# One graph-attention kernel: decoding of the next group, the last product of a group and two element-wise operations moved in the order of work

## The chip, the cores and the metric

The kernel runs on one core of a Trainium2 chip. The metric is the device time in microseconds (us) of one execution. The engines are TensorE (PE in the rows; PEld is its loading of weights), VectorE (DVE), ScalarE (ACT), GpSimd (POOL) and SyncE (SP), which only starts transfers here. Each follows its own list of instructions in order, and they meet at semaphores: an instruction that waits holds up all that is behind it on its engine.

## The reference

```python
scores = (x @ W @ a1)[:, None] + (ent @ W @ a2)[None, :]      # 4096 x 4096
e = where(scores > 0, scores, 0.2 * scores)
e = where(adj > 0, e, -9e15)                                  # adj: int32, 4096 x 4096
h = softmax(e, axis=1) @ ent + x                              # 4096 x 64
out = layernorm(x + elu(h))                                   # over the last axis
```

## The kernel before, in words

The 4096 rows of x are cut into five groups of 4, 6, 8, 8 and 6 tiles of 128 rows; the 4096 entities are 32 blocks of 128. A *step* is one block b of one group g; there are 160 steps. I name a group g0 to g4 and a block b0 to b31. Every group goes through these stages, spread over the group before it and itself:

- **Turning.** GpSimd starts the loads of `adj` (four blocks of a group in one load, five buffers `raw`). TensorE turns two blocks at a time (`turn_pair`, L693) into one of two `pairs` buffers in PSUM. ScalarE, for some pairs VectorE, stores them as `mask` (L315, L511); 44 blocks of mask are kept, so turning runs ahead of the group that uses it. From b20 of group g on, the pairs turned belong to group g+2.
- **Histogram and decoding.** Every stored pair also goes through small matmuls into `hist` (`add_hist`, L709). Once all 16 pairs of the next group are in, ScalarE copies hist (`copy_hist`, L323), TensorE spreads it (`spread_hist`, L724), VectorE finds each row's highest bin and a shift (`decode`, nine instructions from L480 to L500), TensorE makes a row of it (`make_row`, L731), and ScalarE copies the row to `drow` (`take_row`, L340). The first hist matmul of the group after next waits for the copy. The first `masked` of the next group waits for `drow`.
- **Weights.** For two blocks at a time VectorE takes the minimum of mask and drow (`masked`, L522, into `xm`), one block at a time it adds the score (`exponents`, L530), and ScalarE takes the exponential (`weights`, L329). Five buffers `wts` let VectorE be at most four blocks ahead of TensorE.
- **Product.** `weigh` (L744 and L747) multiplies the weights with the entities and sums them, three steps (LAG) behind: at b of the program TensorE does the product of block b-3. One product is eight L744 and six or eight L747 matmuls. The first product of a group waits until ScalarE has copied the sums of the group before (`take_acc`, L348 and L349, at b2).
- **Finish.** Sums and rows are turned back (`turn_sums`, L762; `turn_back`, L772), and VectorE works through twelve parts (`finish`) of the group before, one at some blocks: sum and reciprocal, entity features, multiply, add x, minimum with 0 (L584) and maximum (L585), add ScalarE's exponential (L589), mean (L592), centring (L595), square (L598), sum of squares (L601), scale (L604), and after a power on GpSimd (L272) the last multiplication (L607).

Which part stands at which block is set by the table of numbers at the top of the file. Ahead of the loop stands a prologue: scale and highest value of the scores, then all turning and decoding of g0. In it VectorE reduces the entities (`ent_part`, L615) and then does `find_shift` (L465 to L470), which waits for a small matmul (`p_to_all`, L677); behind both stand its first stored pairs (L511), for which TensorE's later turns wait.

Of the kernel before, what the change touches and what calls it, by code (L numbers as in the profile page):

```python
# [9 lines left out]
NG = len(SIZES)  # L10
# [41 lines left out]
def attention_layernorm(nc, x, adj, ent_blocks, turned_in, weights_in, out):  # L52

# [17 lines left out]
    with ctx:  # L71
# [133 lines left out]
        rstd_done = sem("rstd_done")  # L205
        y_done = sem("y_done")
# [53 lines left out]
        def _(pool):  # L260
# [37 lines left out]
        def _(act):  # L298
# [32 lines left out]
            def elu(g):  # L331
                e_g = e[:, 0:SIZES[g], :]
                act.wait_ge(att_done, g + 1)
                act.activation(e_g, e_g, ACT.Exp).then_inc(elu_done, 1)  # L334
# [21 lines left out]
            for j in range(4, GROUP_PAIRS):  # L356
                store_pair(j)
                if j == 10:
                    p_row(0)
# [3 lines left out]
            for g in range(NG):  # L363
                for b in range(NB):
                    s = NB * g + b
                    if g and b == ACC_AT:
                        take_acc(g - 1)
                    for j in range(made_by(s - 1), made_by(s)):
# [3 lines left out]
                    if g and b == ELU_AT:  # L372
                        elu(g - 1)
                    if g + 1 < NG and b == HIST_COPY_AT:
                        copy_hist(g + 1)
                    if g + 1 < NG and b == DROW_AT:
                        take_row(g + 1)
                    weights(g, b)
            take_acc(NG - 1)
            elu(NG - 1)  # L380

        @block.vector
        def _(dve):
# [184 lines left out]
            def finish(g, part):  # L568
# [10 lines left out]
                elif part == 3:  # L579
                    fin_wait()  # L580
                    fin_inc(dve.tensor_tensor(y_g, y_g, x_gr, ALU.add))
                elif part == 4:
                    fin_wait()
                    dve.tensor_scalar(e_g, y_g, 0.0, None, ALU.min).then_inc(att_done, 1)  # L584
                    fin_inc(dve.scalar_tensor_tensor(y_g, y_g, 0.0, x_gr, ALU.max, ALU.add))  # L585
                elif part == 5:
                    fin_wait()
                    dve.wait_ge(elu_done, g + 1)
                    fin_inc(dve.scalar_tensor_tensor(y_g, e_g, -1.0, y_g, ALU.add, ALU.add))  # L589
# [3 lines left out]
                elif part == 7:  # L593
                    fin_wait()
                    fin_inc(dve.scalar_tensor_tensor(y_g, spread(mean), -1.0 / F, y_g, ALU.mult, ALU.add))  # L595
                elif part == 8:
                    fin_wait()
                    fin_inc(dve.tensor_tensor(e_g, y_g, y_g, ALU.mult))  # L598
                elif part == 9:
                    fin_wait()  # L600
                    fin_inc(dve.tensor_reduce(var[:, 0:n], e_g, AX.X, ALU.add))  # L601
                elif part == 10:
                    fin_wait()
                    dve.tensor_scalar(var[:, 0:n], var[:, 0:n], 1.0 / F, EPS, ALU.mult, ALU.add).then_inc(var_done, 1)  # L604
                else:
# [240 lines left out]
```

## Time and profile before

| | us |
|---|---|
| median of 3 runs | 375.44 (375.23 to 376.32) |
| the profiled execution | 377.46 |
| its span, first to last instruction | 375.4 |
| PE busy | 305.7 (81%) |
| DVE busy | 308.4 (82%) |
| ACT busy | 264.4 (70%) |
| POOL busy | 47.2 (13%) |

The profiled execution took 377.46 us, 2.0 us more than its span. The span divides by the first `masked` of each group: the prologue ends at 45.12 us, g0 at 101.3, g1 at 166.41, g2 at 239.53, g3 at 307.0, and g4 with the rest runs to the end. No engine is busy all the time, but two are above 80%, so what counts is who is waited for in each stage. The granted TensorE clock (PEclk) is 1.00 at the full 2.4 GHz and 0.50 at 1.2 GHz.

### The profile page before, as it was taken

Reading aid. Unit: us, or ns where it says so; the run is one execution under the profiler, and the core shown is the slowest. Engines: PE = TensorE matmul, PEld = TensorE weight load, DVE = VectorE, ACT = ScalarE, POOL = GpSimd, SP = SyncE. Lnnn points to the kernel's source line nnn. Section 1 sums busy time; section 2 is a strip of 40 time slices with the busy share of each in tenths; the row PEclk is TensorE's granted clock in tenths of the full one; section 3 lists DMA queues with packets and bytes.
Section 4 is the critical chain, followed back from the end, with each engine's and each line's share of the span. In section 5 each row is a group of like instructions: output and inputs, shape, how many; then the busy total and the mean of one; then the engine's idle time right before and its main releaser. Section 6 shows DMA issues by size and latency. Waiting matters only on the chain.

```text
span 375.4 us, 9071 instructions
## 1 busy us (share of the span) xinstructions
PE 305.7 (81%) x3920; PEld 163.2 (43%) x3920; DVE 308.4 (82%) x436; ACT 264.4 (70%) x263; POOL 47.2 (13%) x54
## 2 busy tenths in 40 slices
PE   1379599997879999996999979879997767957750
PEld 0356466665545554552545435335442313412220
DVE  1894586863797999569899996799999999999955
ACT  1163299897588989589999975799876568646530
POOL 5012111110101001400100041000000500000201
PEclk9999879998989999998999989999999999999995
DMA  7999999999977940999665009940000000000000
GB/s 151 251 206 174 186 200 161 205 207 208 188 119 115 151 74 2 144 208 209 103 91 81 0 3 168 205 72 0 2 2 2 2 28 3 3 0 2 0 30 22
DMA packets 35240, 37.32 MB, mean 99 GB/s; under 512 B 832, under 2 KB 34432, under 8 KB 35200
## 3 DMA queue, kind: packets, MB, share of 16 engines
q0 software_dynamic: 33408, 33.56, 56.3%
q1 hardware_dynamic: 1792, 3.18, 3.0%
q8 instruction: 31, 0.51, 0.5%
q14 instruction: 9, 0.07, 0.1%
HBM read 69.24 MB, written 1.05 MB: 187 GB/s over the span
## 4 chain that ended last, share of the span: by engine, by line
PE 35%; DVE 27%; issue 23%; ACT 11%; DMA 2%; POOL 1%; POOLq 0%; DVEq 0%; SPq 0%; ACTq 0%
PE acc L744 13%; PE pairs L693 10%; DVE xm L522 8%; DVE wts L530 7%; PE acc L747 6%; ACT mask L315 5%; ACT wts L329 3%; PE hist L709 3%; DMA ent_sb<-ent_blocks_dram 2%; DVE y L563 1%; PE misc L668 1%; ACT drow L340 1%; DVE ent_part L615 1%; PE misc L724 1%; POOL rstd L272 1%
## 5 line engine op out<-in xcount | busy, mean ns | idle before, releaser
L329 ACT ACTIVATE wts<-wts,q_bias 128x768 f32<-128x768 f32 (+2 forms) x160 | 152.1, 976 | 56.1 <-DVE wts L530 55.9
L744 PE MATMUL acc<-wts,ent_sb 128*32 128x384 f32 (+2 forms) x1280 | 152.5, 525 | 28.3 <-ACT wts L329 19.4
L530 DVE SCALAR_TENSOR_TENSOR wts<-pb,q_bend,xm 128x768 f32<-128x768 f32 (+2 forms) x160 | 167.5, 1070 | 8.2 <-PE acc L747 7.7
L315 ACT ACTIVATE mask<-pairs 128x2048 bf16<-128x2048 bf16 (+2 forms) x67 | 104.3, 1559 | 35.8 <-PE pairs L693 35.5
L747 PE MATMUL acc<-wts,onesf 128*32 128x256 f32 (+1 forms) x1152 | 93.2, 362 | 0.0
L522 DVE TENSOR_TENSOR xm<-mask,drow 128x1536 bf16<-128x1536 bf16 (+2 forms) x80 | 80.8, 1010 | 9.9 <-ACT drow L340 9.9
L693 PE MATMUL pairs<-ident,raw 128*128 128x128 bf16 x1024 | 79.5, 235 | 1.8 <-ACT mask L315 0.9
L693 PEld LDWEIGHTS pairs<-ident,raw 128*128 128x128 bf16 x1024 | 65.2, 106 | 27.9 <-issue 27.5
L747 PEld LDWEIGHTS acc<-wts,onesf 128*32 128x32 f32 x1152 | 41.7, 112 | 71.3 <-issue 66.0
L744 PEld LDWEIGHTS acc<-wts,ent_sb 128*32 128x32 f32 x1280 | 34.7, 109 | 57.7 <-ACT wts L329 43.3
L266 POOL DMA_DIRECT2D raw<-adj_dram x40 | 33.4, 836 | 153.9 <-PE pairs L693 151.3
L709 PE MATMUL hist<-mask,codes 128*32 128x384 bf16 (+2 forms) x320 | 34.9, 357 | 8.6 <-ACT acc_sb L323 5.5
L272 POOL TENSOR_TENSOR rstd<-var,mhalf 128x6 f32<-128x6 f32 (+2 forms) x5 | 12.7, 2535 | 170.5 <-DVE var L604 170.5
L511 DVE TENSOR_SCALAR mask<-pairs 128x1024 bf16<-128x1024 bf16 (+2 forms) x13 | 11.9, 916 | 13.2 <-PE pairs L693 13.2
L709 PEld LDWEIGHTS hist<-mask,codes 128*32 128x32 bf16 x320 | 10.4, 97 | 18.2 <-ACT mask L315 9.2
L480 DVE SCALAR_TENSOR_TENSOR above<-misc,steps_key 128x192 f32<-128x192 f32 (+2 forms) x5 | 1.9, 374 | 15.0 <-PE misc L724 15.0
L652 PE MATMUL misc<-identf,qm 128*2 128x128 f32 x2 | 0.6, 398 | 9.6 <-DVE qm L407 9.6
L340 ACT ACTIVATE drow<-misc 128x768 bf16<-128x768 bf16 (+2 forms) x5 | 4.2, 843 | 3.5 <-PE misc L731 3.5
L563 DVE SCALAR_TENSOR_TENSOR y<-ent_sum,empty,misc 128x64 f32<-128x64 f32 x32 | 6.6, 280 | 0.0
L668 PE MATMUL misc<-identf,pcol 128*128 128x128 f32 x32 | 6.0, 317 | 0.0
L399 DVE TENSOR_TENSOR wts<-ent_sb,wa_row 128x2048 f32<-128x2048 f32 x1 | 2.3, 2293 | 4.1 <-DMA ent_sb<-ent_blocks_dram 4.1
L334 ACT ACTIVATE e<-e 128x384 f32<-128x384 f32 (+2 forms) x5 | 2.7, 535 | 3.9 <-DVE e L584 3.9
(99 smaller groups left out, 107.8 us busy)
## 6 DMA issues: line engine op xcount, KB each, us to landing
raw<-adj_dram POOLq DMA_DIRECT2D x16, 1024.0 KB, 12.2
raw<-adj_dram POOLq DMA_DIRECT2D x16, 768.0 KB, 10.6
raw<-adj_dram POOLq DMA_DIRECT2D x8, 512.0 KB, 10.2
ent_sb<-ent_blocks_dram SPq DMA_DIRECT2D x1, 1024.0 KB, 7.5
x_sb<-x_dram SPq DMA_DIRECT2D x2, 256.0 KB, 8.4
out_dram<-y SPq DMA_DIRECT2D x2, 256.0 KB, 2.0
x_sb<-x_dram SPq DMA_DIRECT2D x2, 192.0 KB, 8.2
out_dram<-y SPq DMA_DIRECT2D x2, 192.0 KB, 4.6
```

The lines of the kernel that those rows point to most:

```text
L266: pool.dma_start(raw[:, n % RAWS, 0:SIZES[g], :], rows(adj, g)[:, :, P * CHUNK * c:P * CHUNK * (c + 1)]).then_inc(adj_in[n % RAWS], 16)
L272: pool.tensor_tensor(rstd[:, 0:n], var[:, 0:n], mhalf[:, 0:n], ALU.pow).then_inc(rstd_done, 1)
L315: act.activation(mask[:, i % RING:i % RING + 2, 0:n], pairs[j % 2][:, :, 0:n], ACT.Relu, scale=2.0 ** LIFT).then_inc(act_mask_done, 1)
L329: act.activation(part, part, ACT.Exp, bias=q_bias[:, b:b + 1]).then_inc(w_done, 1)
L511: dve.tensor_scalar(mask[:, i % RING:i % RING + 2, 0:n], pairs[j % 2][:, :, 0:n], 2.0 ** LIFT, 0.0, ALU.mult, ALU.max).then_inc(dve_mask_d ...
L522: dve.tensor_tensor(xm[:, i % XS:i % XS + 2, 0:n], mask[:, i % RING:i % RING + 2, 0:n], drow[:, g % 2, 0:n].unsqueeze(1).to_broadcast([P, ...
L530: dve.scalar_tensor_tensor(wts[:, i % SLOTS, 0:n], pb[:, P * TILE0[g]:P * TILE0[g] + n], q_bend[:, b:b + 1], xm[:, i % XS, 0:n], ALU.max, ...
L563: ins = dve.scalar_tensor_tensor(y[:, t, :], ent_sum[:, 0:F], empty[:, row:row + 1], misc[:, features_at(g, t)], ALU.mult, ALU.add)
L693: ins = pe.transpose(pairs[j % 2][:, k, P * t:P * t + P], raw[:, n % RAWS, t, at:at + P], ident[:, :])
L709: ins = pe.matmul(hist[to:to + Q, 0:n], codes[:, i % NB, :], mask[:, i % RING, n * c:n * c + n], start=(pair == 0), stop=(pair == GROUP_PA ...
L744: pe.matmul(acc[0][to:to + Q, 0:n], ent_sb[:, b, Q * f:Q * f + Q], part[:, n * k:n * k + n], start=(b == 0), stop=(b == NB - 1))
L747: ins = pe.matmul(acc[1][Q * k:Q * k + Q, 0:P * m], onesf[:, 0:Q], part[:, P * t:P * t + P * m], start=(b == 0), stop=(b == NB - 1))
```

## The change

The groups, buffers and mathematics are the same. What moves:

- TensorE adds the last histogram pair at b22 (before at b23), ScalarE copies hist at b23 (24), TensorE spreads it at b24 behind its product (27, ahead of it), and makes the row at b27 behind its product (30, ahead of it). ScalarE takes the row at b28 ahead of storing a pair (30, behind it). `decode` stays at b27 on VectorE.
- The last product of a group (block 31) stands ahead of the turns and histogram of b2 (before behind them).
- The sums are turned at b5 (6); the finish parts sit at b7, 12, 13, 14, 18 to 21, 25, 26 and 30.
- elu's exponential reads y itself, without the minimum with 0 ahead of it; VectorE afterwards takes the minimum of the exponential with 1. The -1 is left out, since the layernorm removes a constant. The maximum with 0 now waits for the exponential.
- The squares are taken by ScalarE (b22) and no longer by VectorE.
- The GpSimd power of g0 and g1 stands four loads later in its list.
- In the prologue `find_shift` stands ahead of the reduction `ent_part` (before behind it).

```diff
-TURN_SUMS_AT = 6
+HIST_END = 22
+TURN_SUMS_AT = 5
-ELU_AT = 18
-HIST_COPY_AT = 24
-SPREAD_AT = 27
+ELU_AT = 15
+SQUARE_AT = 22
+HIST_COPY_AT = 23
+SPREAD_AT = 24
 DECODE_AT = 27
-ROW_AT = 30
-DROW_AT = 30
-FINISH_AT = {8: 0, 13: 1, 14: 2, 15: 3, 16: 4, 20: 5, 21: 6, 22: 7, 23: 8, 24: 9, 25: 10, 29: 11}
+ROW_AT = 27
+DROW_AT = 28
+FINISH_AT = {7: 0, 12: 1, 13: 2, 14: 3, 18: 4, 19: 5, 20: 6, 21: 7, 25: 8, 26: 9, 30: 10}
...
-                if n == NB // CHUNK * (deviations + 1) + (24 + RING) // CHUNK + 1:
+                if n == (NB * (deviations + 1) + 28 + RING) // CHUNK + RAWS - 1:
                     deviation(deviations)
...
-                act.activation(e_g, e_g, ACT.Exp).then_inc(elu_done, 1)
+                act.activation(e[:, 0:n, :], y[:, 0:n, :], ACT.Exp).then_inc(elu_done, 1)
+            def squares(g):
+                n = SIZES[g]
+                act.wait_ge(centred, g + 1)
+                act.activation(e[:, 0:n, :], y[:, 0:n, :], ACT.Square).then_inc(square_done, 1)
...
                 elif part == 4:
-                    fin_wait()
-                    dve.tensor_scalar(e_g, y_g, 0.0, None, ALU.min).then_inc(att_done, 1)
+                    dve.wait_ge(att_done, g + 1)
+                    dve.wait_ge(elu_done, g + 1)
                     fin_inc(dve.scalar_tensor_tensor(y_g, y_g, 0.0, x_gr, ALU.max, ALU.add))
                 elif part == 5:
                     fin_wait()
-                    dve.wait_ge(elu_done, g + 1)
-                    fin_inc(dve.scalar_tensor_tensor(y_g, e_g, -1.0, y_g, ALU.add, ALU.add))
+                    fin_inc(dve.scalar_tensor_tensor(y_g, e_g, 1.0, y_g, ALU.min, ALU.add))
...
                 elif part == 8:
-                    fin_wait()
-                    fin_inc(dve.tensor_tensor(e_g, y_g, y_g, ALU.mult))
+                    dve.wait_ge(square_done, g + 1)
+                    fin_inc(dve.tensor_reduce(var[:, 0:n], e_g, AX.X, ALU.add))
...
             p_highest()
+            find_shift()
             dve.wait_ge(const_done, 4)
             dve.tensor_reduce(ent_part[:, :], ent_sb[:, :, :].rearrange("p b f -> p f b"), AX.X, ALU.add).then_inc(part_done, 1)
-            find_shift()
...
+                    if g and b == LAG - 1:
+                        weigh(g - 1, NB - 1)
                     for j in range(made_by(s - 1), made_by(s)):
                         turn_pair(j)
-                    hist_to(made_by(s - HIST_LAG))
+                    hist_to(min(made_by(s), GROUP_PAIRS * (g + 2)) if b == HIST_END else made_by(s - HIST_LAG))
...
+                    if s >= LAG and not (g and b == LAG - 1):
+                        weigh(*divmod(s - LAG, NB))
                     if g + 1 < NG and b == SPREAD_AT:
                         spread_hist(g + 1)
                     if g + 1 < NG and b == ROW_AT:
                         make_row(g + 1)
-                    if s >= LAG:
-                        weigh(*divmod(s - LAG, NB))
```

On TensorE, from the spreading to the making of the row towards the end of g1 (L724 spreads and L731 makes the row; L693 are turns, L709 histogram, L744 with L747 one product), before:

```order
L724 MATMUL misc<-stack,acc_sb 128x64 x4
L744 MATMUL acc0<-wts,ent_sb 32x384 x4
L747 MATMUL acc1<-wts,onesf 32x256 x3
L693 MATMUL pairs1<-ident,raw 128x128 x16
L744 MATMUL acc0<-wts,ent_sb 32x384 x4
L747 MATMUL acc1<-wts,onesf 32x256 x3
L709 MATMUL hist<-mask,codes 32x512 x4
L744 MATMUL acc0<-wts,ent_sb 32x384 x4
L747 MATMUL acc1<-wts,onesf 32x256 x3
L693 MATMUL pairs0<-ident,raw 128x128 x16
L731 MATMUL misc<-ident,dcol 128x128 x8
```

The same engine and place after, where L736 spreads and L743 makes the row, L705 are turns, L721 histogram, L756 with L759 one product:

```order
L736 MATMUL misc<-stack,acc_sb 128x64 x4
L721 MATMUL hist<-mask,codes 32x512 x4
L756 MATMUL acc0<-wts,ent_sb 32x384 x4
L759 MATMUL acc1<-wts,onesf 32x256 x3
L705 MATMUL pairs0<-ident,raw 128x128 x16
L756 MATMUL acc0<-wts,ent_sb 32x384 x4
L759 MATMUL acc1<-wts,onesf 32x256 x3
L721 MATMUL hist<-mask,codes 32x512 x4
L756 MATMUL acc0<-wts,ent_sb 32x384 x4
L759 MATMUL acc1<-wts,onesf 32x256 x3
L743 MATMUL misc<-ident,dcol 128x128 x8
```

In both, three products stand between the two, but the spreading now follows the product of block 21 and the row that of block 24; before, they preceded those of blocks 24 and 27.

TensorE again, at b2 and b3 of g2, where the products of g1 (384 wide) end and those of g2 (512 wide) begin, before:

```order
L693 MATMUL pairs0<-ident,raw 128x128 x16
L744 MATMUL acc0<-wts,ent_sb 32x384 x4
L747 MATMUL acc1<-wts,onesf 32x256 x3
L709 MATMUL hist<-mask,codes 32x512 x4
L744 MATMUL acc0<-wts,ent_sb 32x512 x4
L747 MATMUL acc1<-wts,onesf 32x256 x4
```

And after:

```order
L756 MATMUL acc0<-wts,ent_sb 32x384 x4
L759 MATMUL acc1<-wts,onesf 32x256 x3
L705 MATMUL pairs0<-ident,raw 128x128 x16
L721 MATMUL hist<-mask,codes 32x512 x4
L756 MATMUL acc0<-wts,ent_sb 32x512 x4
L759 MATMUL acc1<-wts,onesf 32x256 x4
```

The last product of g1 has moved ahead of the turns, so that turns and histogram lie between it and the first product of g2.

VectorE in the prologue, from the highest value of p to the first stored pairs (L460 `p_all`, L615 `ent_part`, L465 to L470 `find_shift`), before:

```order
L460 TENSOR_REDUCE p_all<-misc 1x1
L615 TENSOR_REDUCE ent_part<-ent_sb 128x65
L465 TENSOR_SCALAR reach<-misc,qg 128x1
L466 TENSOR_SCALAR shift<-qg 128x1
L468 SCALAR_TENSOR_TENSOR shift<-reach,shift 128x1
L470 TENSOR_SCALAR q_bias<-qcol,shift 128x32
L511 TENSOR_SCALAR mask<-pairs1 128x2x512 x5
```

And after:

```order
L475 TENSOR_REDUCE p_all<-misc 1x1
L480 TENSOR_SCALAR reach<-misc,qg 128x1
L481 TENSOR_SCALAR shift<-qg 128x1
L483 SCALAR_TENSOR_TENSOR shift<-reach,shift 128x1
L485 TENSOR_SCALAR q_bias<-qcol,shift 128x32
L628 TENSOR_REDUCE ent_part<-ent_sb 128x65
L526 TENSOR_SCALAR mask<-pairs1 128x2x512 x5
```

The reduction of the entities has moved behind the four small operations.

## Rows read from the trace of the kernel before

**Rows 1.** Busy time of g1, g2 and g3.

```profile
core 0: us, PE busy (x) PEld busy (x) DVE busy (x) ACT busy (x) POOL busy (x), PEclk, DMA share, GB/s
101.30:166.41 65.11, 60.69 (x820) 34.15 (x816) 54.14 (x77) 54.26 (x52) 9.64 (x10) 0.97 0.71 115
166.41:239.53 73.12, 67.32 (x833) 32.58 (x827) 65.07 (x77) 62.87 (x54) 8.90 (x9) 0.95 0.67 105
239.53:307.00 67.47, 56.10 (x692) 24.36 (x692) 66.27 (x79) 52.11 (x49) 4.96 (x1) 1.00 0.16 29
```

**Rows 2.** The same columns, for the end of each group into the next.

```profile
85.00:109.00 24.00, 18.69 (x305) 12.27 (x305) 15.21 (x27) 16.64 (x21) 2.64 (x3) 0.93 1.18 193
148.00:174.50 26.50, 21.61 (x280) 11.52 (x282) 18.88 (x28) 20.60 (x21) 6.14 (x6) 0.99 1.02 168
218.00:248.00 30.00, 23.76 (x281) 10.91 (x277) 23.85 (x31) 21.63 (x21) 6.44 (x6) 0.94 0.87 138
221.38:224.79 3.41, 3.41 (x26) 1.32 (x27) 3.24 (x3) 2.04 (x2) 3.41 (x3) 0.53 0.00 0
```

**Rows 3.** Waits: engine and line, waited for, total us, times, longest.

```profile
DVE above L480 <- PE misc L724: 15.0, 4, 5.9
PE acc L744 <- ACT wsum_sb L349: 8.7, 4, 2.7
```

**Rows 4.** Timeline, end of g2: start, us, instruction, idle before it.

```profile
221.38 0.35 PE L709 MATMUL hist<-mask,codes 128*32 128x384 bf16 x4 [2.24 <-ACT acc_sb L323]
221.54 1.89 PE L744 MATMUL acc<-wts,ent_sb 128*32 128x512 f32 x8
226.94 1.10 PE L724 MATMUL misc<-stack,acc_sb 128*128 128x64 f32 x8
228.09 0.43 DVE L480 SCALAR_TENSOR_TENSOR above<-misc,steps_key 128x256 f32<-128x256 f32 x1 [3.47 <-PE misc L724]
230.61 2.48 DVE L530 SCALAR_TENSOR_TENSOR wts<-pb,q_bend,xm 128x1024 f32<-128x1024 f32 x2
239.53 1.23 DVE L522 TENSOR_TENSOR xm<-mask,drow 128x2048 bf16<-128x2048 bf16 x1 [2.44 <-ACT drow L340]
247.56 1.06 PE L744 MATMUL acc<-wts,ent_sb 128*32 128x512 f32 x8 [2.70 <-ACT wsum_sb L349]
248.99 0.84 PE L693 MATMUL pairs<-ident,raw 128*128 128x128 bf16 x12
```

**Rows 5.** Timeline, first products of g1 and g2.

```profile
108.80 1.41 PE L744 MATMUL acc<-wts,ent_sb 128*32 128x384 f32 x8 [1.78 <-ACT wsum_sb L349]
174.16 1.93 PE L744 MATMUL acc<-wts,ent_sb 128*32 128x512 f32 x8 [2.41 <-ACT wsum_sb L349]
```

**Rows 6.** Timeline, prologue.

```profile
25.79 3.85 DVE L615 TENSOR_REDUCE ent_part<-ent_sb 128x65 f32<-128x2080 f32 x1
27.95 0.58 PE L677 MATMUL misc<-p_all,onesf 1*128 1x1 f32 x2
30.20 0.68 DVE L511 TENSOR_SCALAR mask<-pairs 128x1024 bf16<-128x1024 bf16 x1
31.04 1.01 PE L693 MATMUL pairs<-ident,raw 128*128 128x128 bf16 x8 [0.87 <-DVE mask L511]
```

**Rows 7.** Timeline, the wait for drow at g4, and finish parts.

```profile
307.00 0.96 DVE L522 TENSOR_TENSOR xm<-mask,drow 128x1536 bf16<-128x1536 bf16 x1 [0.89 <-ACT drow L340]
334.03 0.42 DVE L584 TENSOR_SCALAR e<-y 128x512 f32<-128x512 f32 x1
...
346.73 0.70 DVE L598 TENSOR_TENSOR e<-y 128x512 f32<-128x512 f32 x1
...
367.02 0.52 ACT L334 ACTIVATE e<-e 128x384 f32<-128x384 f32 x1 [3.94 <-DVE e L584]
369.42 0.56 DVE L598 TENSOR_TENSOR e<-y 128x384 f32<-128x384 f32 x1
```

**Rows 8.** Page, part 5: the power on GpSimd, with count, busy, mean ns.

```profile
L272 POOL TENSOR_TENSOR rstd<-var,mhalf 128x6 f32<-128x6 f32 (+2 forms) x5 | 12.7, 2535 | 170.5 <-DVE var L604 170.5
```

More of the change, by code:

```diff
@@ L205, in attention_layernorm @@
         rstd_done = sem("rstd_done")
+        centred = sem("centred")
+        square_done = sem("square_done")
         y_done = sem("y_done")
@@ L357, in _ @@
                 store_pair(j)
-                if j == 10:
+                if j == FIRST_ROW_AT + 1:
                     p_row(0)
@@ L367, in _ @@
                         take_acc(g - 1)
+                    if g + 1 < NG and b == DROW_AT:
+                        take_row(g + 1)
                     for j in range(made_by(s - 1), made_by(s)):
@@ L373, in _ @@
                         elu(g - 1)
+                    if g and b == SQUARE_AT:
+                        squares(g - 1)
                     if g + 1 < NG and b == HIST_COPY_AT:
                         copy_hist(g + 1)
-                    if g + 1 < NG and b == DROW_AT:
-                        take_row(g + 1)
                     weights(g, b)
@@ L380, in _ @@
             elu(NG - 1)
+            squares(NG - 1)
         @block.vector
@@ L580, in finish @@
                     fin_wait()
-                    fin_inc(dve.tensor_tensor(y_g, y_g, x_gr, ALU.add))
+                    dve.tensor_tensor(y_g, y_g, x_gr, ALU.add).then_inc(att_done, 1)
                 elif part == 4:
-                    fin_wait()
-                    dve.tensor_scalar(e_g, y_g, 0.0, None, ALU.min).then_inc(att_done, 1)
+                    dve.wait_ge(att_done, g + 1)
+                    dve.wait_ge(elu_done, g + 1)
                     fin_inc(dve.scalar_tensor_tensor(y_g, y_g, 0.0, x_gr, ALU.max, ALU.add))
@@ L594, in finish @@
                     fin_wait()
-                    fin_inc(dve.scalar_tensor_tensor(y_g, spread(mean), -1.0 / F, y_g, ALU.mult, ALU.add))
+                    dve.scalar_tensor_tensor(y_g, spread(mean), -1.0 / F, y_g, ALU.mult, ALU.add).then_inc(centred, 1)
                 elif part == 8:
-                    fin_wait()
-                    fin_inc(dve.tensor_tensor(e_g, y_g, y_g, ALU.mult))
+                    dve.wait_ge(square_done, g + 1)
+                    fin_inc(dve.tensor_reduce(var[:, 0:n], e_g, AX.X, ALU.add))
                 elif part == 9:
-                    fin_wait()
-                    fin_inc(dve.tensor_reduce(var[:, 0:n], e_g, AX.X, ALU.add))
-                elif part == 10:
                     fin_wait()
@@ L605, in finish @@
                 else:
+                    dve.wait_ge(centred, g + 1)
                     dve.wait_ge(rstd_done, g + 1)
@@ L635, in _ @@
                         if b == NB - 2:
-                            dve.wait_ge(p_rows, 8)
+                            dve.wait_ge(p_rows, ROWS)
                         masked(s // 2 + 1)
-            for part in range(12):
+            for part in range(11):
                 finish(NG - 1, part)
@@ L719, in spread_hist @@
                 if g == 1:
-                    pe.wait_ge(p_rows, 8)
+                    pe.wait_ge(p_rows, ROWS)
                 if g >= 2:
@@ L790, in _ @@
                     p_to_all()
-                if j == 9:
+                if j == FIRST_ROW_AT:
                     p_row(0)
```

4 lines of the change are left out of this document (3 added, 1 removed).

## The prediction, as it was put on record before the changed kernel ran

> **What bounds the kernel now.** I read the busy time by group first, then the ends of the groups, then the waits, and last the timeline at the places the waits point to.
>
> By group [rows 1], g1 and g2 keep TensorE at 60.69 of 65.11 us and 67.32 of 73.12 us, VectorE at 54.14 and 65.07. g3 is another case: VectorE is busy 66.27 of 67.47 us, and TensorE only 56.10. So up to the end of g2 TensorE sets the pace, with VectorE close behind in g2; in g3 VectorE does.
>
> The ends of the groups show where TensorE loses [rows 2]: 24.00 - 18.69 = 5.31 us idle from g0 to g1, 26.50 - 21.61 = 4.89 from g1 to g2, 30.00 - 23.76 = 6.24 from g2 to g3, together 16.4 us. The waits name the chain [rows 3]: VectorE waits 15.0 us in four places for the spreading before it can decode, and TensorE waits 8.7 us for the copy of the old sums. The timeline at the end of g2 has it piece by piece [rows 4]. TensorE stands 2.24 us at a histogram matmul because ScalarE's copy of hist comes late. The spreading, three steps on, lets VectorE stand 3.47 us ahead of decode (228.09). After decoding, exponents come late, the row comes three steps on, the first minimum of g3 stands 2.44 us for drow (239.53), ScalarE is late with the copy of the sums, and TensorE stands 2.70 us (247.56). The same last wait is 1.78 us at g1 and 2.41 us at g2 [rows 5].
>
> There is a second price. Behind the 2.24 us wait TensorE ran at 1.2 GHz (granted clock 0.53 over 3.41 us [rows 2]); the eight L744 of a product took 1.89 us there and 1.06 us at full clock [rows 4]. A stretch of 3.41 us then holds 3.41 x 1.06 / 1.89 = 1.9 us of full-clock work, so it costs 1.5 us. I count four such stretches: inside the window of g0 to g1 (0.93 over 24 us, as 1.7 / 24 = 0.07), behind 108.80 (1.41 us for a smaller product), behind 174.16 (1.93 us), and at 221.38. The Trainium skill ("TensorE: Matmul & The Clock Gate", on the throttle metric) counts a throttled time times one half, so 1.7 us a stretch, 6.8 in all; the rows give 6.0, since part of the work isn't array time. I use the rows.
>
> **The change part by part.**
>
> *Decoding chain and last product.* TensorE's waste around the three ends is 5.31 + 3.0 = 8.3 us, 4.89 + 1.5 = 6.4, and 6.24 + 1.5 = 7.7: 22.4 us. I work out one end in the new order, g2 to g3. The product of block 21 ends at 221.38 - 2.24 = 219.14. One product takes 248.99 - 247.56 = 1.43 us, the turns of two blocks 0.84, a histogram pair 0.35, the spreading 1.10 [rows 4], the row some 0.6 (eight transposes against twelve in 0.84). From there to the first product of g3 stand the spreading, six histogram pairs, five turns, ten products and the row: 1.10 + 2.1 + 4.2 + 14.3 + 0.6 = 22.3, so 241.4 in place of 247.56, 6.2 us earlier. For it ScalarE must have the copy of hist by 220 (it now stands two instructions earlier, ahead of the store and the exponential of b24) and the copy of the sums by 241.4; the turns of b2 and one histogram pair, 1.2 us, now cover the latter. I leave 0.4 us for ScalarE.
>
> The new order puts one wait in: the row, behind block 24's product, waits for decode. TensorE gets there at 219.14 + 1.10 + 2 x 0.35 + 3 x 1.43 + 0.84 = 226.1. VectorE reached decode at 228.09 - 3.47 = 224.6, some 0.9 us earlier without the two removed operations, and decoding takes 230.61 - 228.09 = 2.5 us, so 226.2 to 227.1. TensorE waits 0.1 to 1.1 us; I take 0.6. Behind the row are queued turns, histogram and products of blocks 25 and 26, whose weights are ready; VectorE may be four blocks ahead, so it isn't held by this. Net 5.2 us for g2 to g3, against the waste of 7.7 a ratio of 0.8 before the row's wait. With this 0.8 the others give 6.7 and 5.1; in g1 VectorE has more slack (54 of 65 us), so I add no wait there. Gain 17.0 us; ends for the range: half of it (8.5) and all of the waste (22.4).
>
> *Finish.* VectorE loses the minimum (0.42 for a group of 8) and the square (0.70) [rows 7]; issued back to back they weigh about 1.0 us. In g3 and g4 VectorE is the bound, so this counts twice: 2.0 us. In g1 and g2 TensorE covers it, 0. The wait of 0.89 us for drow at g4 goes, since the row is there two steps earlier: 0.9 us. ScalarE gets five squares. At equal size its exponential took 0.52 us and VectorE's square 0.56 [rows 7]; I take 0.5 to 0.6 a square. They hide behind VectorE in g3 and g4; in g2 ScalarE is busy 62.87 of 73.12 us, and I let one count: 0.5 us lost. The maximum and the square behind the exponential now wait across engines; three blocks lie between in the loop.
>
> The Trainium skill ("ScalarE: Activation LUTs", Rules for kernel authors) speaks against the squares: element-wise products belong on VectorE, up to three times faster in bf16. By that a square would take 3 x 0.56 = 1.7 us on ScalarE, and the tail would be 1.2 us longer than below. These operands are fp32, and the row of ScalarE's 0.52 us at the same size says otherwise.
>
> *Tail.* Nothing covers there. The minimum goes (some 0.3 us, from the 0.42 of the larger one), the maximum (about as long as a square, 0.56) is no longer beside the exponential, and the square changes engine with two hand-overs of about 0.1: 0.3 us lost. Bounds 0 and 1.0.
>
> *Prologue.* Here the change costs. Before, VectorE filled the wait for p_to_all with the reduction of the entities, 25.79 to 29.64; the matmul it waits for ends at 27.95 + 0.58 = 28.5, hidden. After, it stands idle from about 25.8 to 28.6, does find_shift (30.20 - 29.64 = 0.6) and only then the reduction, 3.8 us, so the stored pair of 30.20 comes at 33.0. TensorE already waited for exactly this pair (31.04, idle 0.87) [rows 6], and all behind it in the prologue is a chain up to the first weights. So 2.8 us later. Bounds: 1.5 if the later pairs catch up, 4.5 if TensorE, idle 3.7 us, is granted its full clock later.
>
> *The rest.* Turning of sums one step earlier, other blocks for the parts, loads: 0, as TensorE or VectorE does the same work beside it. The GpSimd power comes behind a load (below).
>
> Sum on the profiled execution: 377.46 - 17.0 - 2.0 - 0.9 + 0.5 + 0.3 + 2.8 = 361.2 us. It stood 2.0 us above the median of the runs, so the median should come to 359.1; I say 359.
>
> **The rivals.**
>
> 1. *VectorE takes the place of TensorE in g1 and g2.* For it: in g2 VectorE has only 73.12 - 65.07 = 8.05 us idle, and part must stay. The power, now behind the load that waits for the turns of b28, takes 2.5 us [rows 8] behind that load, and VectorE asks for it at b30, where it can be two blocks ahead: up to 2 us in each of two groups. Against: one of ten operations is gone, and TensorE has three products in between. If the last two ends gain 3 us each in place of 5.1 and 5.2, that is 4.3 more, with part of the power's wait 6: 365 us.
>
> 2. *All the waste goes*, since ratios from one walk are rough: 5.4 us better, 353.7 us. Against it: ScalarE is near its own limit in g2.
>
> 3. *Slower: the row holds TensorE.* Decode stays at b27, but the row now stands behind block 24's product. If VectorE begins decoding only when TensorE has come to the row, TensorE idles the whole 2.5 us, and, with VectorE an exponent pair behind (2.5 + 1.2), 6.2 us; its clock falls behind that for 1.5: 7.7 us at each of three ends, 23 us against the 22.4 of now. With the prologue's 2.8, the tail and the square, less 2.9, it comes to 377 us. It decides from a decode that begins 2 to 4 us after 224.6. Against it: before, VectorE was there 3.47 us too early.
>
> 4. *The prologue alone is mis-sized*, from 357.8 to 360.8: inside the forecast's range.
>
> **How the numbers follow.** The forecast, 355.5 to 362.5 us, gets 0.60; rival 1 (to 368) 0.24; rival 2 0.10; rival 3 0.05. Of rival 1 a little and of the rest 0.01 could end within 0.3% of 375.4, about what a measurement of this kernel can tell from no change. The range 354 to 366 leaves out some of rivals 1 and 2 and all of 3. Faster 0.93, same 0.03, slower 0.04.
>
> **What would show it.** Right: no wait of TensorE's histogram for the hist copy; VectorE's waits for the spreading down from 15.0 to under 3 us (one of the four is the prologue's and stays); TensorE's wait for the sums' copy under 3 us; no stretch at half clock around g1, g2 and g3; the first minimum of g0 near 48 us in place of 45.12; about 1 us less VectorE work in each of g3 and g4. Wrong: TensorE waiting more than 2 us at the row, VectorE waiting for the power at b30, a first minimum still at 45, or a length of g1 or g2 unchanged with VectorE busy throughout.

## The result, and the profile after

| | median, us | runs | profiled execution, us | its span, us |
|---|---|---|---|---|
| before | 375.49 | 4 (375.23 to 376.32) | 377.46 | 375.4 |
| after | 354.06 | 4 (353.69 to 354.47) | 354.47 | 352.4 |

The ratio is 0.9426 (95% interval 0.9408 to 0.9444): 5.7% faster, 21.4 us between the medians and 23.0 between the two profiled executions. I had forecast 359 with a range from 354. The direction and the mechanism were right, the size too small. The time lies at the range's edge, just inside it in us and just outside it as a ratio to the kernel before (354 / 375.44 = 0.9429), where my rival 2 stood (353.7).

The first minimum of each group, from the timelines, gives the groups:

| stretch | before | after | difference | forecast |
|---|---|---|---|---|
| prologue | 45.12 | 48.05 | +2.9 | +2.8 |
| g0 | 56.18 | 48.42 | -7.8 | -6.7 |
| g1 | 65.11 | 58.07 | -7.0 | -5.1 |
| g2 | 73.12 | 65.20 | -7.9 | -4.7 |
| g3 | 67.47 | 65.55 | -1.9 | -1.9 |
| g4 and tail | 68.4 | 67.2 | -1.3 | -0.7 |

The boundary between g1 and g2 is VectorE's. In the changed kernel VectorE waits 1.6 us for the power shortly before it (below), so g1 looks that much longer and g2 shorter than on TensorE; their sum isn't touched by this.

The windows of the changed kernel for g1, g2, g3 (they answer to [rows 1]) and for one stretch in g3; the columns are those of [rows 1]:

```profile
96.47:154.54 58.07, 57.55 (x826) 33.69 (x822) 53.66 (x76) 54.43 (x54) 8.06 (x9) 1.00 1.02 164
154.54:219.74 65.20, 64.80 (x849) 32.66 (x845) 64.02 (x76) 62.74 (x55) 8.93 (x9) 1.00 0.75 113
219.74:285.29 65.55, 58.59 (x724) 26.23 (x720) 65.24 (x78) 54.08 (x51) 4.64 (x2) 0.97 0.13 22
278.09:281.50 3.41, 2.59 (x18) 1.08 (x22) 3.31 (x7) 1.42 (x2) 0.00 (x0) 0.53 0.02 5
```

TensorE is idle 0.52 us in the whole of g1 and 0.40 in g2, where the ends alone had cost it 4.89 and 6.24 [rows 2], and its granted clock is 1.00 throughout both. From the start of g1 to the last product the only half-clock stretch is the last row's, in g3. The half-clock stretch of 6.8 us at the start of g0 (granted clock 0.50 from 46.2 us) was there before too, from 44.1 us.

The waits of the changed kernel (they answer to [rows 3]; same columns):

```profile
DVE above L495 <- PE misc L736: 1.5, 1, 1.5
PE acc L756 <- ACT wsum_sb L361: 3.0, 3, 1.9
PE misc L743 <- DVE dcol L515: 7.0, 3, 4.4
DVE y L619 <- POOL rstd L279: 3.1, 2, 1.6
DVE reach L480 <- PE misc L689: 2.7, 1, 2.7
PE pairs L705 <- DVE mask L526: 3.7, 1, 3.7
```

VectorE's wait for the spreading fell from 15.0 us to the prologue's 1.5, and TensorE's for the sums from 8.7 to 3.0. Four waits are new or larger: TensorE for the row, VectorE for the power, and in the prologue VectorE for the small matmul and TensorE for the stored pair. Of VectorE's two waits for the power only the first is new, at b30 of g1. The second stands in the tail, where the kernel before had it too:

```profile
153.27 0.42 DVE L619 TENSOR_TENSOR y<-y,rstd 128x256 f32<-128x256 f32 x1 [1.61 <-POOL rstd L279]
349.62 0.56 DVE L619 TENSOR_TENSOR y<-y,rstd 128x384 f32<-128x384 f32 x1 [1.51 <-POOL rstd L279]
```

The end of g2 on the timeline of the changed kernel, to be read against [rows 4]:

```profile
205.21 1.07 PE L756 MATMUL acc<-wts,ent_sb 128*32 128x512 f32 x8
206.63 1.10 PE L736 MATMUL misc<-stack,acc_sb 128*128 128x64 f32 x8
207.67 0.35 PE L721 MATMUL hist<-mask,codes 128*32 128x384 bf16 x4
210.61 0.42 DVE L495 SCALAR_TENSOR_TENSOR above<-misc,steps_key 128x256 f32<-128x256 f32 x1
213.28 0.62 PE L743 MATMUL misc<-ident,dcol 128*128 128x128 bf16 x8 [0.32 <-DVE dcol L515]
219.74 1.22 DVE L537 TENSOR_TENSOR xm<-mask,drow 128x2048 bf16<-128x2048 bf16 x1
...
223.13 0.34 PE L721 MATMUL hist<-mask,codes 128*32 128x384 bf16 x4
223.29 1.04 PE L756 MATMUL acc<-wts,ent_sb 128*32 128x512 f32 x8
224.58 1.04 PE L756 MATMUL acc<-wts,ent_sb 128*32 128x512 f32 x8
225.99 0.84 PE L705 MATMUL pairs<-ident,raw 128*128 128x128 bf16 x12
226.76 0.35 PE L721 MATMUL hist<-mask,codes 128*32 128x384 bf16 x4
227.76 1.06 PE L756 MATMUL acc<-wts,ent_sb 128*32 128x512 f32 x8 [0.66 <-ACT wsum_sb L361]
```

The histogram matmul no longer waits, decode (210.61) starts on VectorE's own account 3.98 us after the spreading began, the row waits 0.32 us, the first minimum of g3 has no wait, and the wait for the sums is 0.66 in place of 2.70. From the end of block 21's product (taken as the start of the spreading) to the first product of g3 it is 227.76 - 206.63 = 21.1 us; before it was 247.56 - 219.14 = 28.4.

The prologue of the changed kernel, against [rows 6]:

```profile
28.62 0.22 DVE L480 TENSOR_SCALAR reach<-misc,qg 128x1 f32<-128x1 f32 x1 [2.72 <-PE misc L689]
29.28 3.85 DVE L628 TENSOR_REDUCE ent_part<-ent_sb 128x65 f32<-128x2080 f32 x1
33.04 0.68 DVE L526 TENSOR_SCALAR mask<-pairs 128x1024 bf16<-128x1024 bf16 x1
33.87 1.01 PE L705 MATMUL pairs<-ident,raw 128*128 128x128 bf16 x8 [3.65 <-DVE mask L526]
```

This part made the kernel slower, as worked out: the stored pair comes at 33.04 (forecast 33.0), 2.84 us late.

### The profile page after: what moved, and what is told of

The parts are those of the page before. It is cut to its first block, busy times and chain, and to the rows that moved or that the text cites. A ratio compares the mean times of both kernels' runs of the same rounds, so it can differ in the third digit from the quotient of the medians.

```text
span 352.4 us, 9071 instructions
## 1 busy us (share of the span) xinstructions
PE 297.7 (84%) x3920; PEld 161.4 (46%) x3920; DVE 304.1 (86%) x426; ACT 265.0 (75%) x268; POOL 46.2 (13%) x54
## 4 chain that ended last, share of the span: by engine, by line
PE 42%; DVE 26%; issue 22%; ACT 6%; DMA 2%; POOL 1%; POOLq 0%; DVEq 0%; SPq 0%; ACTq 0%
PE acc L756 15%; PE pairs L705 13%; DVE xm L537 10%; PE acc L759 7%; DVE wts L545 5%; PE hist L721 3%; ACT mask L322 3%; DMA ent_sb<-ent_blocks_dram 2%; ACT wts L336 2%; PE misc L680 1%; DVE y L578 1%; DVE ent_part L628 1%; POOL rstd L279 1%; PE misc L736 1%; DVE wts L414 1%
## 5 line engine op out<-in xcount | busy, mean ns | idle before, releaser
L756 PE MATMUL acc<-wts,ent_sb 128*32 128x384 f32 (+2 forms) x1280 | 150.5, 518 | 12.0 <-ACT wts L336 8.6
L759 PE MATMUL acc<-wts,onesf 128*32 128x256 f32 (+1 forms) x1152 | 91.2, 356 | 0.0
L705 PE MATMUL pairs<-ident,raw 128*128 128x128 bf16 x1024 | 77.2, 231 | 5.1 <-DVE mask L526 3.7
L705 PEld LDWEIGHTS pairs<-ident,raw 128*128 128x128 bf16 x1024 | 63.2, 103 | 28.5 <-issue 28.1
L759 PEld LDWEIGHTS acc<-wts,onesf 128*32 128x32 f32 x1152 | 40.8, 111 | 70.2 <-issue 64.7
L756 PEld LDWEIGHTS acc<-wts,ent_sb 128*32 128x32 f32 x1280 | 36.0, 109 | 38.5 <-ACT wts L336 21.4
L721 PE MATMUL hist<-mask,codes 128*32 128x384 bf16 (+2 forms) x320 | 34.3, 356 | 2.3 <-ACT mask L322 1.0
L279 POOL TENSOR_TENSOR rstd<-var,mhalf 128x6 f32<-128x6 f32 (+2 forms) x5 | 11.6, 2318 | 118.2 <-DVE var L615 118.2
L721 PEld LDWEIGHTS hist<-mask,codes 128*32 128x32 bf16 x320 | 10.1, 97 | 10.0 <-issue 2.0
L743 PE MATMUL misc<-ident,dcol 128*128 128x128 bf16 x32 | 3.2, 248 | 7.0 <-DVE dcol L515 7.0
L743 PEld LDWEIGHTS misc<-ident,dcol 128*128 128x128 bf16 x32 | 2.1, 109 | 8.7 <-DVE dcol L515 8.1
```

The source lines that it names most:

```text
L279: pool.tensor_tensor(rstd[:, 0:n], var[:, 0:n], mhalf[:, 0:n], ALU.pow).then_inc(rstd_done, 1)
L705: ins = pe.transpose(pairs[j % 2][:, k, P * t:P * t + P], raw[:, n % RAWS, t, at:at + P], ident[:, :])
L721: ins = pe.matmul(hist[to:to + Q, 0:n], codes[:, i % NB, :], mask[:, i % RING, n * c:n * c + n], start=(pair == 0), stop=(pair == GROUP_PA ...
L756: pe.matmul(acc[0][to:to + Q, 0:n], ent_sb[:, b, Q * f:Q * f + Q], part[:, n * k:n * k + n], start=(b == 0), stop=(b == NB - 1))
L759: ins = pe.matmul(acc[1][Q * k:Q * k + Q, 0:P * m], onesf[:, 0:Q], part[:, P * t:P * t + P * m], start=(b == 0), stop=(b == NB - 1))
```

## The experiments

Ratios are to the kernel before on the same chip in the same rounds, with 95% intervals. The kernel before itself spread from 372.8 to 378.9 us over these runs, so steps between two changed versions are read from their medians; in seven of the eleven versions the runs agree within about 1 us (in `a_split` but for one run). The versions ran on three chips, where the kernel before had medians of 375.8 us (`b_shift_early`, `b_chain`, `b_chain_last`, `a_shift_late`), 373.9 us (`b_hist`, `b_hist_spread`, `a_sq_dve`, `a_row_g3`) and 376.2 us (`a_power`, `a_split`, `a_split_power`). A step between medians of two chips is therefore uncertain by one or two us, and a step of 0.5 us isn't told by them. The stage lengths in the traces tell more: g0 took 48.41 to 48.43 us in all seven traces of the changed kernel and its variants, on whatever chip. The prologue is less steady: with `find_shift` in its old place it ended between 44.23 and 45.16 us.

Together the first runs build the change up part by part.

**The first link alone** (`b_hist`): on the kernel before,

```diff
+HIST_END = 22
...
-HIST_COPY_AT = 24
+HIST_COPY_AT = 23
...
-                    hist_to(made_by(s - HIST_LAG))
+                    hist_to(min(made_by(s), GROUP_PAIRS * (g + 2)) if b == HIST_END else made_by(s - HIST_LAG))
```

> The kernel before with only the first link of the chain moved: last histogram pair at b22, ScalarE's copy of hist at b23; spreading, row and drow where they were. Theory (each link carries its own part of the waste): the waits of TensorE for that copy (5.5 us in three places) and the half-clock stretches behind them go, VectorE's waits for the spreading shrink but don't vanish since TensorE still comes to it at b27; 375.6 - 6 to - 9, about 368 us. Rival (the first link alone releases the rest, since TensorE is then early at everything behind): 360 us or less.

Measured 366.49 us (365.36 to 368.71), ratio 0.9799 (0.9751 to 0.9847), 9 us faster than the usual 375.5 and 7.4 us faster than the kernel before on its own chip: within the theory. TensorE no longer waits for the copy of hist, VectorE's waits for the spreading fall from 15.0 to 6.4 us, and the waits behind stay as they were. In the kernel before:

```profile
PE hist L709 <- ACT acc_sb L323: 5.5, 3, 2.2
DVE xm L522 <- ACT drow L340: 9.9, 5, 3.3
```

And in this version, where the first of these is gone:

```profile
DVE above L481 <- PE misc L725: 6.4, 3, 2.6
DVE xm L523 <- ACT drow L341: 10.1, 5, 3.3
PE acc L745 <- ACT wsum_sb L350: 8.7, 4, 2.7
```

**With the spreading three steps earlier** (`b_hist_spread`):

```diff
-SPREAD_AT = 27
+SPREAD_AT = 24
...
-                    if g + 1 < NG and b == SPREAD_AT:
-                        spread_hist(g + 1)
...
                     if s >= LAG:
                         weigh(*divmod(s - LAG, NB))
+                    if g + 1 < NG and b == SPREAD_AT:
+                        spread_hist(g + 1)
```

> As the run with the first link moved, and the spreading at b24 behind its product; the row stays at b30 ahead of its product, drow at b30 behind the stored pair. Theory (the decoding, which now starts up to 6 us earlier, is the larger part, and the row only gives the last waits for drow): 360 to 362 us. Rival (the row decides): no better than the first link alone, about 367 us, with VectorE's wait for drow up from 2.4 to over 5 us at each group.

Measured 364.65 us (364.03 to 364.77), ratio 0.9739 (0.9704 to 0.9774): 1.8 us more on the same chip, less than the theory's 5. The rival is half right. VectorE's wait for the spreading is gone but for the prologue's, and it turned into a longer wait for drow; the sums are as late as before:

```profile
DVE above L481 <- PE misc L725: 1.5, 1, 1.5
DVE xm L523 <- ACT drow L341: 11.3, 5, 3.7
PE acc L745 <- ACT wsum_sb L350: 8.2, 4, 2.7
```

**The whole chain** (`b_chain`): also row at b27 behind its product, drow at b28 ahead of the stored pair.

```diff
-ROW_AT = 30
-DROW_AT = 30
+ROW_AT = 27
+DROW_AT = 28
...
+                    if g + 1 < NG and b == DROW_AT:
+                        take_row(g + 1)
                     for j in range(made_by(s - 1), made_by(s)):
                         store_pair(j)
...
-                    if g + 1 < NG and b == DROW_AT:
-                        take_row(g + 1)
...
-                    if g + 1 < NG and b == ROW_AT:
-                        make_row(g + 1)
                     if s >= LAG:
                         weigh(*divmod(s - LAG, NB))
                     if g + 1 < NG and b == SPREAD_AT:
                         spread_hist(g + 1)
+                    if g + 1 < NG and b == ROW_AT:
+                        make_row(g + 1)
```

> The kernel before with only the decoding chain moved (last histogram pair at b22, copy at b23, spreading at b24 and row at b27 behind the products, drow at b28); last product, finish and prologue as before. Theory (nearly all waste of TensorE at the group ends hangs on the late decoding, the copy of the sums included, since ScalarE was late for it only because the exponents were): three ends lose about 5 to 6 us each, 375.5 - 17 = 358 us, with 1 to 2 us left at each wait for the sums. Rival (the last product does its own share): the waits for the copy of the sums, 6.9 us at g1 to g3 with two stretches at half clock, stay, and the time is 375.5 - 12 = 363 us or more.

Measured 356.38 us (354.66 to 357.04), ratio 0.9477 (0.9449 to 0.9506). The theory's 358 was 1.6 too high. The row (with the copy to drow behind it) is worth 8.3 us beyond the spreading between the medians, which come from two chips, and 9.4 us over g0 to g3 in the traces (249.3 to 239.9). The rival falls: without touching the last product, TensorE's wait for the sums shrinks as well.

```profile
DVE xm L523 <- ACT drow L341: 1.2, 1, 1.2
PE acc L745 <- ACT wsum_sb L350: 3.3, 4, 1.1
PE misc L732 <- DVE dcol L501: 8.5, 3, 4.4
```

So the late copy of the sums was mostly a consequence of the late row, not a wait of its own.

**Chain and last product** (`b_chain_last`): as before, and

```diff
+                    if g and b == LAG - 1:
+                        weigh(g - 1, NB - 1)
                     for j in range(made_by(s - 1), made_by(s)):
                         turn_pair(j)
...
-                    if s >= LAG:
+                    if s >= LAG and not (g and b == LAG - 1):
                         weigh(*divmod(s - LAG, NB))
```

> As the run with the decoding chain moved, and the last product of a group ahead of the turns of b2 too. Theory: all the waste of the three ends is gone, 375.5 - 21 = 354.5 us; what the last product adds to the chain alone is 1 to 4 us (the turns and a histogram pair, 1.2 us each, now cover the copy). Rival (the finish edits free VectorE in g2 and are needed for it): above 358 us, with VectorE waited for in g2.

Measured 354.02 us (353.67 to 354.67), ratio 0.9423 (0.9409 to 0.9437): 2.4 us more, as the theory has it, and its runs agree within 1.0 us where the chain alone spread over 2.4. In the two traces g0 to g3 are only 1.0 us shorter (239.9 to 238.9); the profiled execution of the chain alone was its fastest, 1.7 us under its median. So the last product's own share is 1.0 to 2.4 us. The rival (the finish edits are needed) falls. With TensorE's order alone the kernel is as fast as the whole change: the finish edits win what the prologue loses.

**The prologue alone** (`b_shift_early`), on the kernel before:

```diff
+            find_shift()
             dve.wait_ge(const_done, 4)
             dve.tensor_reduce(ent_part[:, :], ...)
-            find_shift()
```

> The kernel before with one edit: find_shift ahead of the reduction of the entities. Theory (this part of the change costs time): the first minimum of g0 comes at 48.0 us in place of 45.1 and everything behind shifts with it, 375.5 + 2.8 = 378.3 us, ratio 1.0075. Rival (the later turns or the loads catch up, or the clock gives it back): under 377 us, ratio under 1.004.

Measured 377.41 us (375.81 to 379.04, 10 runs), ratio 1.0041 (1.0011 to 1.0071): slower, by 1.6 us, between the two in time, and its interval holds neither 1.0075 nor 1. The trace has the first minimum at 48.11 us, 3.0 later, as expected; but g0, g1 and g2 are each 1.5 to 1.6 us shorter than in the kernel before (56.18, 65.11 and 73.12 in the table above), with the same instructions in them:

```profile
48.11:102.73 54.62, 51.86 (x870) 36.43 (x871) 38.22 (x63) 46.09 (x55) 8.58 (x10) 0.95 1.19 191
102.73:166.23 63.50, 59.08 (x820) 33.32 (x816) 54.13 (x78) 54.03 (x52) 9.62 (x10) 1.00 0.75 121
166.23:237.82 71.59, 65.80 (x833) 32.30 (x827) 64.80 (x76) 62.36 (x54) 8.88 (x9) 0.98 0.68 107
```

The granted clock of g1 is 1.00 here and 0.97 in [rows 1]. The waits are of the same length, but fewer of them were followed by a half-clock stretch: here the granted clock stays at 1.00 around the ends of g0 and g1, and the one stretch left is that at the end of g2 (0.50 from 220.6 us). That a wait of about 2 us is followed by one in some executions only is read from two traces, not from an experiment of its own; it would explain why the kernel before, with such waits, spread over several us, though `b_hist_spread`, which has some too, spread over only 0.7 in four runs. This stays open.

**The change without its prologue edit** (`a_shift_late`), on the changed kernel the reverse of the last diff.

> The changed kernel with find_shift back behind the reduction. Theory: 354.1 - 2.8 = 351.3 us, the fastest so far, first minimum at 45.1 us. Rival (the earlier start collides with the loads in g0, whose transfers are busy more than nine tenths there): 352.5 to 354 us, with TensorE waiting for adj.

Measured 351.49 us (351.19 to 351.79), ratio 0.9355 (0.934 to 0.9371): the theory, to 0.2 us. TensorE never waits for adj. The prologue edit costs the changed kernel 2.6 us. Against the chain with the last product, on the same chip, the finish edits are worth 354.02 - 351.49 = 2.5 us; I had forecast 1.2 (2.0 less 0.5 for ScalarE and 0.3 in the tail). The stage lengths by the first minimum of each group, here and in the versions that are compared with it, show where:

| version | prologue | g0 | g1 | g2 | g3 | g4 and tail |
|---|---|---|---|---|---|---|
| `b_chain_last` | 44.64 | 48.41 | 56.44 | 67.54 | 66.51 | 68.43 |
| `a_shift_late` | 44.79 | 48.43 | 58.06 | 65.19 | 65.55 | 67.18 |
| `a_sq_dve` | 45.16 | 48.42 | 58.06 | 65.77 | 66.29 | 68.32 |
| `a_row_g3` | 45.04 | 48.42 | 58.07 | 65.17 | 65.92 | 67.17 |
| `a_power` | 44.81 | 48.41 | 56.65 | 66.37 | 65.55 | 67.18 |
| `a_split` | 43.53 | 48.42 | 58.05 | 65.18 | 65.55 | 67.17 |

The finish edits take 1.0 us off g3 and 1.2 off g4 with the tail, as forecast, and 0.7 off g1 and g2 together, where I had forecast none and charged 0.5 for ScalarE. The 0.7 has its place: decoding now comes earlier, and TensorE's wait for the row in g2 falls from 1.83 us (`b_chain_last`) to 0.32 (changed kernel):

```profile
210.80 0.62 PE L732 MATMUL misc<-ident,dcol 128*128 128x128 bf16 x8 [1.83 <-DVE dcol L501]
```

**Squares on VectorE again** (`a_sq_dve`), against `a_shift_late`:

```diff
-                    if g and b == SQUARE_AT:
-                        squares(g - 1)
...
-            squares(NG - 1)
...
                     dve.scalar_tensor_tensor(y_g, spread(mean), ...).then_inc(centred, 1)
+                    dve.wait_ge(centred, g + 1)
+                    dve.tensor_tensor(e_g, y_g, y_g, ALU.mult).then_inc(square_done, 1)
```

> The changed kernel with find_shift back behind the reduction, and the squares on VectorE again (at the part of centring, back to back with it). Theory (VectorE is the bound in g3 and g4 and near it in g2): 0.6 us more in each of g3 and g4 and up to 0.5 in g2, tail 0.2 less: 351.5 + 1.3 = 352.8 us. Rival (squares cost ScalarE as much as they save VectorE in g1 and g2): 351.5 us, no change.

Measured 353.89 us (353.12 to 354.13), ratio 0.9451 (0.9417 to 0.9486): 2.4 us slower between the medians, which come from two chips, and 2.8 us in the traces; more than the theory's 1.3, and the rival falls. Its g3 and g2, to be read against 65.55 and 65.20 above:

```profile
217.41:283.70 66.29, 58.59 (x712) 26.07 (x708) 65.94 (x79) 53.65 (x50) 4.63 (x2) 0.95 0.13 22
151.64:217.41 65.77, 64.79 (x849) 32.65 (x845) 64.56 (x76) 62.54 (x54) 8.91 (x9) 1.00 0.74 112
```

So the squares cost 0.7 us in g3 and 0.6 in g2, and nothing in g1. In g2 the cost is TensorE's wait for the row, 0.91 us in place of 0.32. In g4 they cost another 0.7 us up to VectorE's last `exponents`. The other 0.4 us of g4 and tail lie behind VectorE's last operation (2.66 us to the end in place of 2.27) and have no cause in the trace that I can name, and 0.4 us are the unsteady prologue's. The tail's own finish parts take 9.25 us with the square on VectorE and 9.22 with it on ScalarE, so the 0.2 that the theory saw there isn't found. ScalarE took the squares at no cost, in g2 too, where I had charged 0.5.

**The row of g3 back at b30** (`a_row_g3`), against `a_shift_late`:

```diff
-                    if g + 1 < NG and b == ROW_AT:
+                    if g + 1 < NG and b == (30 if g == NG - 2 else ROW_AT):
...
-                    if g + 1 < NG and b == DROW_AT:
+                    if g + 1 < NG and b == (30 if g == NG - 2 else DROW_AT):
```

> The changed kernel with find_shift back behind the reduction, and in g3 alone the row at b30 behind its product and drow at b30 ahead of the store. In the changed kernel TensorE waits 4.4 us for the row in g3 and runs at half clock behind it. Theory (VectorE sets the pace there, so this wait costs nothing): 351.5 us, within 0.4. Rival (the wait and the half clock hold back products that VectorE needs): 349 to 350 us.

Measured 352.01 us (351.63 to 352.12), ratio 0.9403 (0.9363 to 0.9442): 0.5 us more and not less. The wait it addresses is this one, of the changed kernel (the first two rows); the third row is of this version:

```profile
278.91 0.82 PE L743 MATMUL misc<-ident,dcol 128*128 128x128 bf16 x6 [4.37 <-DVE dcol L515]
279.67 1.94 PE L756 MATMUL acc<-wts,ent_sb 128*32 128x512 f32 x8
278.24 1.71 PE L756 MATMUL acc<-wts,ent_sb 128*32 128x512 f32 x8 [3.13 <-ACT wts L336]
```

The wait for the row is gone, but TensorE now stands 3.13 us at the weights instead and again runs at half clock behind it; its idle time in g3 fell only from 6.96 to 6.54 us. That is what to expect where VectorE sets the pace: VectorE is idle 0.31 us in the 65.55 of g3. The later copy to drow made it wait 0.28 us more, and g3 came out 0.4 us longer. So 4.4 us of idle TensorE cost nothing there.

**The power one load earlier** (`a_power`), against `a_shift_late`:

```diff
-                if n == (NB * (deviations + 1) + 28 + RING) // CHUNK + RAWS - 1:
+                if n == (NB * (deviations + 1) + 28 + RING) // CHUNK + RAWS - 2:
```

> The changed kernel with find_shift back behind the reduction, and GpSimd's power of g0 and g1 one load earlier in its list (ahead of the load that waits for the turns of b28). Theory (TensorE is the bound in g1 and g2, so VectorE's two waits of 1.5 us for the power are hidden): 351.5 us, within 0.4. Rival (VectorE is so near the bound that they come through, 3 us in all): 349 to 350 us.

Measured 350.98 us (350.72 to 351.52), ratio 0.9354 (0.9301 to 0.9406): 0.5 us less, which medians of two chips don't tell apart. The expectation counted two waits; the edit can only act on the one in g1, since the other stands in the tail, and it is the one that goes. In the table above g1 is 1.4 us shorter and g2 1.2 us longer: VectorE passes the boundary earlier and then waits for TensorE. So of the wait of 1.6 us all but 0.2 was hidden behind TensorE. In my rival 1 this wait stood for 1.7 of its 6 us.

**The reduction in two halves** (`a_split`), against `a_shift_late`: features 0 to 32 where the whole stood, 33 to 64 behind the second stored pair.

```diff
-            dve.tensor_reduce(ent_part[:, :], ...).then_inc(part_done, 1)
+            dve.tensor_reduce(ent_part[:, 0:33], ...).then_inc(part_done, 1)
...
                 store_pair(j)
+                if j == 9:
+                    dve.tensor_reduce(ent_part[:, 33:FA], ...).then_inc(part_done, 1)
...
-                pe.wait_ge(part_done, 1)
+                pe.wait_ge(part_done, 2)
```

> The changed kernel with find_shift behind the first half of the reduction of the entities and the second half behind the second stored pair of VectorE. Theory (the first half, 1.9 us, fills the wait for p_to_all of 2.7 us, so that find_shift starts at 28.6 and the first stored pair at 29.3 in place of 30.2; TensorE waited 0.87 us for it, and the second half lies in a wait of 2.8 us): 351.5 - 0.9 = 350.6 us. Rival (the second half delays a later pair, or two short reductions cost more than one): 351.5 us or more.

Measured 350.14 us (three runs from 349.75 to 350.21, and one of 498.18 at a mean granted clock of 0.59), ratio 0.9325 (0.9237 to 0.9413): 1.3 us less, a little over the theory's 0.9; in the trace too the prologue is 1.3 us shorter (43.53 for 44.79) and nothing else moves. The first half fills the wait for the small matmul, and the second lies in the next gap:

```profile
25.74 2.02 DVE L627 TENSOR_REDUCE ent_part<-ent_sb 128x33 f32<-128x1056 f32 x1
28.52 0.22 DVE L480 TENSOR_SCALAR reach<-misc,qg 128x1 f32<-128x1 f32 x1 [0.77 <-PE misc L691]
29.18 0.68 DVE L526 TENSOR_SCALAR mask<-pairs 128x1024 bf16<-128x1024 bf16 x1
31.73 1.97 DVE L632 TENSOR_REDUCE ent_part<-ent_sb 128x32 f32<-128x1024 f32 x1
```

**Both** (`a_split_power`): the edits of the last two together.

> Both of the two others in one kernel: reduction in two halves, and the power one load earlier. Theory: as with the two halves alone, 350.6 us, since the power's wait is hidden. Rival: 349 us or less if the waits for the power come through once the rest is tighter.

Measured 349.61 us (349.24 to 351.67), ratio 0.9327 (0.9263 to 0.939). This is the fastest version: 4.5 us below the changed kernel. By the medians 2.6 of this are the prologue edit taken back, 1.3 the halves and 0.5 the power; the traces give the power 0.2.

## Why the prediction was right or wrong

- **What bounds the kernel.** Right. TensorE paced up to the end of g2, and removing its waste shortened the kernel by about as much; VectorE paced g3 and g4. In g2 the two are now close: VectorE is busy 64.02 of 65.20 us.
- **Decoding chain and last product.** The mechanism was right and the term mis-sized: 17.0 us on record, 22.0 measured over g0 to g2 without the finish edits (`b_chain_last`) and 22.7 with them. The step that failed is the walk from block 21's product to g3's first one, and with it the ratio of 0.8 that I carried to the other two ends. I added each instruction group's own duration. But they overlap: histogram to next product is 223.29 - 223.13 = 0.16 us, not 0.35; turns take 226.76 - 225.99 = 0.77, not 0.84; a product followed by a product 224.58 - 223.29 = 1.29, one followed by turns 225.99 - 224.58 = 1.41, not 1.43 each. The six histogram pairs alone make 1.1 us of it, and the first two lines of [rows 4] had it already: histogram at 221.38, product at 221.54. The path without waits so came out at 22.3 us where it is 21.1 - 0.98 = 20.1. The two waits I added to it, 0.4 for the sums and 0.6 for the row, came out at 0.66 and 0.32. At this end the path fell by 28.4 - 21.1 = 7.3 us, where I had 5.2.
- **The ratio of 0.8.** There was a slip in it as well: 0.8 is 6.2 / 7.7, without the 0.4 for ScalarE; with it the ratio is 0.75 and the gain on record would have been 0.7 us smaller still. With the right path the ratio would have been 1.0 or so, which is rival 2: the gain is the 22.4 us that I had counted as waste. It deserved more than 0.10, since nothing in the profile said that a part must stay. Not every microsecond is accounted for: from the first minimum of g0 to the first product of g3 TensorE's idle time fell from 16.8 to 2.2 us, which with the four half-clock stretches makes 20.6; some 2 us of the 22.7 I can't assign.
- **Which link carries it.** I worked out the end as one sum. The runs split it, by the medians: first link 7 to 9 us (by which median of the kernel before), spreading 1.8, row 8.3 (10 if the ratios on the two chips are compared), last product 2.4. In the traces g0 to g3 together took 261.9 us before, 251.6 with the first link, 249.3 with the spreading, 239.9 with the row and 238.9 with the last product. Of the first step's 10.3 us, 4.7 are half-clock stretches: `b_shift_early`, without the first link but with one such stretch between 60 us and the end of g2 like `b_hist`, took 257.2.
- **Half-clock stretches.** Their price was right: 1.5 us on record, and 1.5 to 1.6 per group between two traces of one order. The count of four belonged to that execution, which stood 2.0 us above the median; the trace of `b_shift_early` has one. The gain is 23.0 us between the profiles and 21.4 between medians for this reason as far as I can see, but which executions have how many stretches wasn't tested.
- **Row on TensorE (rival 3).** VectorE came to decode early enough: waits of 0.32 us in g2 and none in g0 and g1. In g3 it was 4.4, which I had named as a sign of being wrong; it cost nothing, since VectorE paces g3. Without the finish edits the wait in g2 was 1.83.
- **Finish.** 2.5 us against 1.2, the wait for drow apart. g3 and g4 gave 1.9 of the 2.0 on record. The 0.5 us I charged ScalarE in g2 wasn't paid; VectorE's relief counted in g2 too, through the row.
- **VectorE as the new bound, and the power (rival 1).** The wait for the power at b30, my other sign of being wrong, was there in one group, 1.6 us, and hidden but for 0.2. TensorE stayed the bound.
- **Tail.** 9.0 us from VectorE's first part to its last before, 9.2 after: 0.2 lost against 0.3. From there to the end it took 2.7 us before and 2.3 after, which I hadn't forecast and can't explain.
- **Prologue.** Right to 0.1 us in the trace (2.9); 3.0 and 3.3 us between the traces that differ in this edit alone, 2.6 us in the medians of the changed kernel with and without it.

## What to carry to other kernels

When an engine in bound stretches loses time to a chain of hand-overs, move every link: here the first link and the row carried 7 to 9 and 8 to 10 us, and the spreading between them mostly lengthened the next wait. Add up a path by the distances from start to start, not by durations, and if nothing in the profile says that part of the waste must stay, give the case that all of it goes a large chance; here the gain was as large as the whole of it. A long reduction in front of a wait is cover for it; an edit that puts the wait first pays for both.

## What the runs showed of the hardware that I had not expected

- A wait of some 2 us on TensorE was followed by a stretch at 1.2 GHz in one trace and not in another of the same order around it: the last histogram wait of g0 and the first products of g1 and g2 in the kernel before, but not with the prologue edit alone. The kernel before spread from 372.8 to 378.9 us over 27 runs on three chips, the changed one, whose TensorE hardly waits from g0 to g2, over 0.8 in four runs.
- Half clock in the prologue cost next to nothing. From 22 to 40 us of the prologue the granted clock was 0.53 in the trace of `b_shift_early` and 1.00 in that of the changed kernel, with the same order there; their first minima came at 48.11 and 48.05 us. With `find_shift` in its old place the three traces with such a stretch had it at 44.88 to 45.16 us, the six others at 44.23 to 45.12.
- A square of 128x384 fp32 takes ScalarE 0.52 us and VectorE 0.56; only one table load (1283 ns) stands in either trace, so no reload came with the squares.
